# Cross-attention and ternary FFN block: context's low part in 64 channels as half passes of K and V, scales spread by transposes

## The reference

```python
x = x + xattn(layernorm(x), ctx)         # (64, 128, 256), (64, 128, 192)
x = x + ffn(layernorm(x))
# xattn: low-rank updates are added to Wq, Wk, Wv, Wo
q = h @ Wq';  k = ctx[:, :124] @ Wk';  v = ctx[:, :124] @ Wv'
ki = ctx[:, 124:] @ Wk_ipa;  vi = ctx[:, 124:] @ Wv_ipa
o = softmax(q k^T / 8) v + softmax(q ki^T / 8) vi      # per head
out = o @ Wo' + bo
# ffn: 8-bit activations, ternary weights
h = depthwise_conv1d(actq(h) @ ternary(w1)^T);  out = actq(silu(h)) @ ternary(w2)^T
```

## Time and profile before

| | us |
|---|---|
| median of 3 runs | 1571.66 |
| lowest, highest | 1570.8, 1572.26 |
| the profiled execution | 1570.99 |
| its span, first to last instruction | 1569.0 |
| PE, DVE, ACT, POOL busy | 1441.2, 1214.9, 1177.5, 660.0 |

### The profile page before, as it was taken

The page is one execution under the profiler, slowest core; times in us unless marked ns, Lnnn a source line. Parts: engine busy times, 40 slices in busy tenths (PEclk is TensorE's granted clock), DMA queues, the critical chain, the costliest instruction groups (busy, mean ns, idle before and its releaser), DMA issues.

```text
span 1569.0 us, 33374 instructions
## 1 busy us (share of the span) xinstructions
PE 1441.2 (92%) x10778; PEld 1174.6 (75%) x10778; DVE 1214.9 (77%) x3059; ACT 1177.5 (75%) x3909; POOL 660.0 (42%) x1058
## 2 busy tenths in 40 slices
PE   7899999999999999999999999999999999998743
PEld 4688788787878878787877878787887878787621
DVE  4364797887879798787969888786978878786966
ACT  3487887968778796978878797887879787787721
POOL 2354444434444443445344444444444344444500
PEclk9999999999999999999999999999999999999965
DMA  9100001000000100000010100000010100000000
GB/s 280 44 30 27 19 15 45 15 29 14 28 29 14 43 14 31 13 28 29 18 38 14 43 0 28 29 28 29 14 43 9 34 14 28 29 1 28 1 14 13
DMA packets 41128, 47.13 MB, mean 30 GB/s; under 512 B 3008, under 2 KB 35200, under 8 KB 41088
## 3 DMA queue, kind: packets, MB, share of 16 engines
q1 hardware_dynamic: 41088, 46.62, 9.8%
HBM read 36.13 MB, written 10.49 MB: 30 GB/s over the span
## 4 chain that ended last, share of the span: by engine, by line
PE 52%; ACT 20%; DVE 19%; issue 9%; DMA 0%; DVEq 0%; ACTq 0%; POOL 0%; SPq 0%; POOLq 0%
PE PS L478 10%; ACT SM L675 8%; PE PS L440 8%; PE PS L491 6%; PE PS L421 5%; PE PS L456 5%; PE PS L465 4%; PE PS L430 4%; PE PS L539 4%; ACT HP L696 2%; DVE GBS L887 2%; PE PS L518 2%; DVE GBS L908 2%; ACT GBS L701 2%; ACT QM L642 2%
## 5 line engine op out<-in xcount | busy, mean ns | idle before, releaser
L1053 POOL TENSOR_TENSOR SM<-SM,RC 128x496 f32<-128x496 f32 (+1 forms) x512 | 331.6, 668 | 747.8 <-DVE RC L822 742.1
L675 ACT ACTIVATE SM<-PS,MX 128x124 f32<-128x124 f32 x1024 | 358.7, 366 | 147.9 <-DVE SM L828 145.8
L478 PE MATMUL PS<-KT,QM 128*128 128x128 f32 x2048 | 278.2, 279 | 29.3 <-ACT SM L675 29.2
L478 PEld LDWEIGHTS PS<-KT,QM 128*128 128x128 f32 x2048 | 249.4, 192 | 44.8 <-ACT SM L675 44.5
L675 ACT ACTIVATION_READ_ACCUMULATOR SM<-PS,MX 128x1 f32 x1024 | 212.9, 208 | 0.0
L1084 POOL TENSOR_TENSOR OTl<-OF,OTh 128x256 fp32r<-128x256 f32 x256 | 196.0, 766 | 14.6 <-ACT OF L669 14.6
L667 ACT ACTIVATE OTh<-PS 128x256 fp32r<-128x256 f32 x256 | 100.4, 392 | 116.3 <-PE PS L456 115.1
L465 PE MATMUL PS<-IDF,SM 128*128 128x128 f32 x1024 | 168.4, 287 | 8.1 <-POOL SM L1053 8.0
L826 DVE TENSOR_REDUCE MX<-PS 128x4 f32<-128x496 f32 x256 | 170.1, 664 | 0.2 <-issue 0.2
L456 PE MATMUL PS<-PT,V 128*64 128x128 f32 x2048 | 168.8, 286 | 0.1
L456 PEld LDWEIGHTS PS<-PT,V 128*64 128x64 f32 x2048 | 106.8, 136 | 81.9 <-issue 74.9
(11 more groups left out here) (142 smaller groups left out, 3566.4 us busy)
## 6 DMA issues: line engine op xcount, KB each, us to landing
XIN<-in_x SPq DMA_DIRECT2D x16, 512.0 KB, 3.6
XRES<-in_x SPq DMA_DIRECT2D x16, 512.0 KB, 3.6
out_y<-HP SPq DMA_DIRECT2D x16, 512.0 KB, 3.0
CRAW<-in_ctxT SPq DMA_DIRECT2D x16, 256.0 KB, 2.7
RRAW<-in_ctxT SPq DMA_DIRECT2D x32, 128.0 KB, 2.9
QM<-in_Wq SPq DMA_DIRECT2D x1, 1024.0 KB, 9.4
GBS<-in_Wo SPq DMA_DIRECT2D x1, 1024.0 KB, 14.1
k_ipa_columns<-HP SPq DMA_DIRECT2D x1, 1024.0 KB, 6.6
```

Of the source, the lines that this page charges most:

```text
L478: m = mm(psS[:, h, :], QM[:, 2 * q + h // 2, h % 2, TOK * b:TOK * b + TOK], KT[:, 2 * q + h // 2, b, :], start=True, stop=True)
L675: m = act.activation(SM[s % 2][:, h, 0:ORG], psS[:, h, 0:ORG], ACT.Exp, bias=MX[s % 2][:, h:h + 1], accum_out=SU[s % 2][:, h:h + 1])
L1053: m = pool.tensor_tensor(part, part, RC[c % 2][:, 4 * i:4 * i + 4].unsqueeze(2).broadcast_to(shape), ALU.mult)
```

## The change

The low part of the 64 channels gets a tile of its own. CTR becomes two tiles: CTR[0] the high part in all 128 rows (the 64 channels twice), CTR[1] the low part in all 128. WKR and WVR become one tile each, of which the 64 rows of one half hold the low part: WKR high in rows 0 to 63 and low in 64 to 127, WVR low in rows 0 to 63 and high in 64 to 127. One full pass with CTR[0] gives high x high and high x low; the missing low x high is a pass over 64 rows only: K's over rows 0 to 63, 512 columns, V's over rows 64 to 127, twice 256 columns. K's half pass is issued with V's unit, right ahead of V's two, and with it the K unit ends there (its unit_full), so ACT's copy of K moves to the half-step behind N_V. The four matmuls of BC1 and BC2 become transposes. The code (line numbers as before):

```diff
-        WKR = [sb(f"WKR{i}", [P, ID], F32R) for i in "hl"]
+        WKR = sb("WKRhl", [P, ID], F32R)
-        WVR = [sb(f"WVR{i}", [P, ID], F32R) for i in "hl"]
+        WVR = sb("WVRlh", [P, ID], F32R)
-        CTR = sb("CTR", [P, T], F32R)
+        CTR = [sb(f"CTR{i}", [P, T], F32R) for i in "hl"]
...
-                        parts = [(WK[0], CTH[0]), (WK[0], CTH[1]), (WK[1], CTH[0]), (WKR[0], CTR), (WKR[1], CTR)]
+                        parts = [(WK[0], CTH[0]), (WK[0], CTH[1]), (WK[1], CTH[0]), (WKR, CTR[0])]
                         for i, (w, c) in enumerate(parts):
-                            m = mm(bank, w[:, tile], c[:], start=(i == 0), stop=(i == 4))
-                        m.then_inc(unit_full, 1)
+                            mm(bank, w[:, tile], c[:], start=(i == 0), stop=False)
                     q = quad_at(n - N_V[a])
                     if q is not None:
                         bank = unit(g, 2 + 6 * q + U_V[a])
                         cols = slice(256 * q, 256 * q + 256)
-                        parts = [(CTH[0], WV[0]), (CTH[1], WV[0]), (CTH[0], WV[1]), (CTR, WVR[0]), (CTR, WVR[1])]
+                        tile = slice(P * (2 * q + a), P * (2 * q + a) + P)
+                        toks = [slice(TOK * (2 * a + b), TOK * (2 * a + b) + TOK) for b in range(2)]
+                        mm(psU[(2 + 6 * q + U_K[a]) % 2], WKR[0:64, tile], CTR[1][0:64, :],
+                           start=False, stop=True).then_inc(unit_full, 1)
                         for b in range(2):
-                            tok = slice(TOK * (2 * a + b), TOK * (2 * a + b) + TOK)
+                            mm(bank[:, 256 * b:256 * b + 256], CTR[1][64:128, toks[b]], WVR[64:128, cols],
+                               start=(b == 0), stop=False, skip_group_check=True)
+                        parts = [(CTH[0], WV[0]), (CTH[1], WV[0]), (CTH[0], WV[1]), (CTR[0], WVR)]
+                        for b in range(2):
                             for i, (c, w) in enumerate(parts):
-                                m = mm(bank[:, 256 * b:256 * b + 256], c[:, tok], w[:, cols], start=(i == 0), stop=(i == 4))
+                                m = mm(bank[:, 256 * b:256 * b + 256], c[:, toks[b]], w[:, cols],
+                                       start=False, stop=(i == 3), skip_group_check=True)
                         m.then_inc(unit_full, 1)
...
-                        m = mm(psF[:, TOK * b:TOK * b + TOK], AD[0][:, b:b + 1].broadcast_to([P, P]), IDF[:], start=True, stop=True)
+                        m = pe.transpose(psF[:, TOK * b:TOK * b + TOK], AD[0][:, b:b + 1].broadcast_to([P, P]), IDF[:])
...
-                        m = mm(psF[:, TOK * b:TOK * b + TOK], AS[1][:, b:b + 1].broadcast_to([P, P]), IDF[:], start=True, stop=True)
+                        m = pe.transpose(psF[:, TOK * b:TOK * b + TOK], AS[1][:, b:b + 1].broadcast_to([P, P]), IDF[:])
...
-                    act.activation(CTR[:], RRAW[:], ACT.Identity).then_inc(c_high, 1)
+                    act.activation(CTR[0][:], RRAW[:], ACT.Identity).then_inc(c_high, 1)
...
-                    q = quad_at(n - N_K[a] - 1)
+                    q = quad_at(n - N_V[a] - 1)
...
-                    dve.tensor_tensor(CTR[64:128, :], RRAW[64:128, :], CTR[64:128, :].bitcast(F32), ALU.subtract).then_inc(c_split, 1)
+                    dve.tensor_tensor(CTR[1][:], RRAW[:], CTR[0][:].bitcast(F32), ALU.subtract).then_inc(c_split, 1)
```

More of the change, by code:

```diff
@@ L297, in program @@
         splits += [(wk_raw, WK[0][:], WK[1][:], 1.0), (wv_raw, WV[0][:], WV[1][:], 1.0),
-                   (wkr_raw, WKR[0][:], WKR[1][:], 1.0), (wvr_raw, WVR[0][:], WVR[1][:], 1.0)]
+                   (wkr_raw, WKR[:], None, 1.0), (wvr_raw, WVR[:], None, 1.0)]
         splits += [(wo_raw[:, 4 * k:4 * k + 4, :], WO[0][:, 4 * k:4 * k + 4, :], WO[1][:, 4 * k:4 * k + 4, :], 1.0) for k in range(2)]
@@ L926, in low_part @@
                 dve.wait_ge(w_high, i + 1)
+                if i == 4:
+                    raw, high, lo_ = raw[64:128, :], high[64:128, :], high[64:128, :]
                 dve.scalar_tensor_tensor(out=lo_, in0=raw, scalar=factor, in1=high.bitcast(F32),
@@ L1066, in _ @@
                 pool.wait_ge(w_high, i + 1)
+                if i == 5:
+                    raw, high, lo_ = raw[0:64, :], high[0:64, :], high[0:64, :]
                 pool.tensor_tensor(lo_, raw, high.bitcast(F32), ALU.subtract).then_inc(wv_low, 1)
```

## The result

The change made the kernel slower: 1651.7 us median (1651.1 to 1652.3) against 1571.2, ratio 1.051, 95% interval 1.049 to 1.053. That is 80.5 us; 65 were forecast.

The account below looks back on a forecast made before the run. PE was taken as busiest (92%), with added waits costing in full where it leads. 4.5 us times 13 groups gave 58, plus 9.5 for groups 0, 1 and 15, less 1.2 and 1.5: +65, so 1636 us, range 1598 to 1664.

Parts of the forecast that it names:

- the three places: Steps 2, 12 and 14 of each group, where the first Q pass was to wait for ACT's late copy of K.
- The moved evacuation: ACT's copy of K behind the exponentials: PE waits of 1.2, 1.3 and 2.1 us, 4.6 us a group.
- pushed copies: Other ACT work delayed by K's copy, before XTh at n = 8 and Q1T at n = 14: 0.1 us each.
- The half passes: K's beside V's in the V unit: 0.33 us, 0.1 over the columns, counted in five of eight V steps, +0.5 a group.
- the cuts: 0.23 us saved per K unit, in odd steps: all in 9 and 15, part in 3 and 13, nothing in 1, 5, 7, 11.
- The 0.1 of s3 and the 0.15 of s13: Savings left from the 0.23 us cut in steps 3 and 13, where PE then waits for DVE's OUTT and for ACT.
- The transposes: BC1 and BC2: nothing gained behind BC1, 0.1 us a group behind BC2, 1.2 us for both at the tail.
- The edges: Groups 0, 1 and 15 add 9.5 us together; the tail's transposes save 1.2 and the first group's projections 1.5.
- PE's busy time: Over the whole kernel, predicted lower by 20 to 40 us in all.
- (3): Rival: DVE and ACT lead in parts of every group, half the stalls are absorbed, 35 us less: 1601; chance 10%.
- (4): Rival: the 2.1 us stall drops PE's clock each time, 2.9 us lost, 15 times: 1680; chance 9%.
- (1): Rival: faster, at best 1531, about 1560 with absorbed steps, if the three waits total under 0.6 us a group; chance 7%.

Follow-up runs that it names:

- e2: The kernel before with all its passes, only ACT's copy of K moved from the half-step behind N_K to the one behind N_V; 1645.8 us.
- e4: The kernel after with each half pass issued twice (K, V, V, K, V, V) ahead of the full passes; 1669.1 us, one run.
- e5: The kernel after without V's two half passes, K's half pass alone; 1649.6 us, one run.
- e7: The kernel after with V's second half pass between its two sets of four full passes; 1683.6 us, one run.
- e1: The kernel before with BC1 and BC2 as transposes and nothing else; 1564.6 us, ratio 0.9956.
- e3: The kernel after with ACT's copy of K put ahead of the same step's exponentials at the three places of the stalls; 1608.3 us.
- e8: The kernel after with the half passes behind the eight full passes of the V unit instead of ahead; 1648.2 us.

## Why the prediction was right, and where its terms were off

The sign, the mechanism, the three places and the range held; the size was 15 us short.

- **The moved evacuation** was put at 1.2 + 1.3 + 2.1 = 4.6 us a group and 0.2 for pushed copies. e2 measures it by itself: 1.31 + 1.49 + 1.78 = 4.58, and +0.21 in the steps around. The sum is right, in part by luck: step 14's part was 0.3 too high, step 12's 0.2 and step 2's 0.1 too low. For step 12 the prediction let the exponentials start 0.47 earlier, because the old K copy ahead of them is gone; step 14 has such a copy too (before, L648 from 851.94 to 852.53), the last exponential piece there starts 3.80 us behind the scores in e2 instead of 4.25, and this 0.45 was left out.
- **The half passes** are the mis-sized term. "Concurrent, with V's half one weight load late", 0.1 over the columns: V's half is not late at all (0.01 us), and the cost is the change of tiling, 0.40 (0.09 in, 0.20 behind the last half pass, 0.11 on the first full pass). The upper bound of 0.43 fits that number, but by luck: it was made of 0.23 for halves one after the other and 0.2 for changes. e4 and e5 refute the first part, and e7 ties the cost to the change and not to the amount. The Trainium skill, "TensorEngine Tiling (Array Packing)", Key Properties, states both that different tiles work in parallel and that a change of mode drains the engine. The trace agrees with both (starts 0.01 us apart, 0.40 us a change), and I had set them against each other where both hold.
- **What of this counts in a group.** Taking e2's and e1's steps off those of the kernel after leaves V steps s3, s6 and s8 at +0.40 or +0.41 and s15 at +0.17, which is a change less a cut of 0.235. The changes in s2 and s14 vanish in the stalls, that of s10 in a wait for DVE (L518, 0.42 us in e2). The pair s11 and s12 adds up to the same in both kernels (1.49 in e2, 1.51 after): the cut brings the scores of step 12 forward by 0.23, but ACT starts its part of the step no earlier (L667 at 883.82 in e2, 6.60 us behind the scores of step 11 in either kernel), and step 12 takes the 0.25 back. So four changes count, where the sum had five. Of the cuts, s9 (-0.24) and s15's came; s11's came to nothing, as predicted. The 0.1 of s3 and the 0.15 of s13 did not come, while s5 (-0.28), costed at nothing, did: the pushed XTh moved its scores 0.45 later, and the wait for ACT at its end (0.34 before) is gone. Together the half-pass design costs some +0.9 a group where -0.21 was in the sum (+0.5 - 0.71). That is 1.1 x 13 = 14 us, nearly the whole miss of the steady groups (58 forecast, 70.7 measured, with 1 us the other way from the transposes).
- **The transposes**: 0.1 a group forecast, 0.2 measured (e1), and nothing behind BC1, as said. At the tail 1.2 was forecast; 1.9 came from BC1 and BC2, and 1.7 from the clock, which no term had.
- **The edges**: -1.5 for the first projections was wrong in sign, and by the prediction's own terms (0.23 less 0.1, six pairs ahead of the first scores) it should have been -0.8. The first scores start 1.6 us later, of which 1.3 lie between the first K pass and the first scores (31.5 us before, 32.8 after; e1, which changes nothing there, 31.5). K's cut comes to nothing there: in each of the last three pairs the V unit then waits longer for ACT's copy of Q (0.35 us instead of 0.12) and starts 1.45 us behind the K unit in both kernels, while the V unit itself takes 1.47 instead of 1.29. Groups 0, 1 and 15 took 12.8 instead of 9.5. There the late copy was undersized and not the half passes: e2 alone took 11.9.
- **PE's busy time** was to fall by 20 to 40 us and rose by 17. Busy time here is the union of listed durations, and those of the half passes (0.50 for a column count that gives 0.40 otherwise) cover the drain. So the waste of a change of tiling does not show as idle time.
- **Rivals.** (3), stalls absorbed, did not come: the steps behind the stall of step 14 gave nothing back in e2 (s15 -0.01, s0 -0.01), and step 13, behind that of step 12, gave back at most 0.16. (4), the clock: it stayed at 1.00 in the group's window above; the waits on K's copy, at most 1.5 us in all groups after and 1.9 in e2, did not lower it. (1) failed at the point named: the three waits together are far over 0.6 us. That bound was also too loose, since it left out the 0.5 of the half passes; with it the sign turns at 0.1.

Additive check, per group: late copy +4.76 (e2), transposes -0.2 (e1), half passes +0.9 by difference, 5.44 by measurement. The last term is worth that little only because waits cover four of the eight changes. In e3, without the stalls, it is 2.67 + 0.20 = 2.87, of which 0.8 is step 13, the later exponentials; some 2.1 are left for the half passes.

The version that beats both kernels is e1, 6.5 us under the kernel before, of which 1.7 is the clock at the tail and may not be its own.

## What to carry to other kernels

Before moving the end of an accumulation, list for its bank who copies it out, in which slot of that engine's program order, and who wants the bank next. A copy that lands behind a step's critical work (here the exponentials), on an engine that works through its program in order, stops the producer until that work is done, and neither engine's busy share warned of it (ACT stood at 75%). Half-array passes side by side are worth it only if enough of them stand together to pay one change of tiling there and back: here 0.40 us was paid to save one 0.235 us pass. When one wait is removed, add the cost of what it had covered.

## What was not expected of the hardware

- Two row halves writing to two banks start 0.01 us apart and keep full pace: doubled half passes add 0.23 us (e4), and V's beside K's add 0.01 (e5).
- Leaving the 64-row tiling costs 0.20 us before the next pass starts, whichever tiling follows (full passes in the kernel after, column halves in e8). It lies inside the listed durations, so it reads as busy.
- An fp32 transpose of 128 x 128 takes 0.124 us a tile, the same spreading as an fp32 product 0.20; at the lower clock level four tiles are listed with 1.1 against 2.1 us.
- At the tail, the second F2 unit ran at the upper clock level (1.92 us) in the kernel after, in e1, e3 and e5 to e8, and at the lower one (3.60) before, in e2 and in e4. The transposes alone do not decide it, since e4 has them. Why the clock rose stays open, and 1.7 us of any comparison of these kernels hang on it.
